# Attention with mixture of experts on one core: attended values kept by feature, normalised by quads of heads, and three rotating PSUM banks

## What is computed

```
xn  = layernorm(x)
Q, K, V = split_heads(xn @ Wq.T), ..., 16 heads of 32
S   = where(causal, Q @ K.T / sqrt(32), -1e30)
att = (softmax(S) @ V, heads side by side) @ Wo.T
ffn = routed experts (2 of 8, width 352) + shared MLP (width 704), both on xn
out = x + att + ffn
```

## Time and profile before

| | us |
|---|---|
| median of 3 runs (1117.13 to 1122.85) | 1117.6 |
| the profiled execution's own time | 1127.01 |
| its span, first to last instruction | 1125.0 |
| PE busy in the span | 1046.2 |
| DVE, ACT, POOL busy | 784.6, 637.9, 506.4 |

### The profile page before, as it was taken

One profiled execution on the slowest core, in us unless ns is written; L12 is line 12 of the kernel. 1 busy time (PEld: TensorE's weight loads), 2 busy tenths in 40 slices (PEclk: granted clock), 3 DMA queues, 4 the chain that ended last, 5 costly groups with the idle time before them and its releaser, 6 DMA issues. The chain is left out here.

```text
span 1125.0 us, 18890 instructions
## 1 busy us (share of the span) xinstructions
PE 1046.2 (93%) x5379; PEld 817.6 (73%) x5380; DVE 784.6 (70%) x1675; ACT 637.9 (57%) x1278; POOL 506.4 (45%) x568
## 2 busy tenths in 40 slices
PE   6999979888899998999999999998989999999994
PEld 4767867666677776777778777776867777778872
DVE  6732324565688887788888888865568888888872
ACT  3323211265588786787787887872155555565550
POOL 0013903388756564556566565651013443333321
PEclk9999989988899999999999999998989999999997
DMA  6989996255543553644445426118789444443432
GB/s 213 322 335 361 136 293 231 94 67 102 132 133 77 150 148 75 163 118 136 115 113 151 126 64 191 45 39 266 243 283 278 90 76 75 75 72 68 71 54 35
DMA packets 106201, 163.61 MB, mean 145 GB/s; under 512 B 53984, under 2 KB 64480, under 8 KB 102656
## 3 DMA queue, kind: packets, MB, share of 16 engines
q1 hardware_dynamic: 95776, 141.82, 44.1%
q0 software_dynamic: 9760, 20.49, 10.0%
q10 hardware_dynamic: 576, 0.26, 0.1%
HBM read 101.25 MB, written 61.28 MB: 144 GB/s over the span
## 5 line engine op out<-in xcount | busy, mean ns | idle before, releaser
L1198 POOL TENSOR_TENSOR prob_lo<-prob,prob_hi 128x512 fp32r<-128x512 f32 (+2 forms) x320 | 308.3, 977 | 203.3 <-ACT prob_hi L1243 147.0
L1236 ACT ACTIVATE prob<-ps_s 128x512 f32<-128x512 f32 (+3 forms) x384 | 188.0, 490 | 127.1 <-PE ps_s L1463 77.1
L1243 ACT ACTIVATE prob_hi<-prob 128x512 fp32r<-128x512 f32 (+3 forms) x384 | 198.6, 517 | 12.4 <-ACT row_stage L1217 12.4
L1862 DVE TENSOR_TENSOR rw_lo<-gu_sb,rw_hi 128x704 fp32r<-128x704 f32 x156 | 138.8, 893 | 52.7 <-ACT rw_hi L1806 47.7
L1306 DVE CUSTOM_DVE_ANT_0 ps_m<-ps_m,causal 128x384 f32<-128x384 f32 (+3 forms) x256 | 126.7, 495 | 69.2 <-PE ps_m L1432 66.9
L1806 ACT ACTIVATE rw_hi<-gu_sb 128x704 fp32r x156 | 123.5, 794 | 62.8 <-PE ps_ru L1895 43.6
L1458 PE MATMUL ps_s<-qs,ks 97*128 97x512 f32 (+3 forms) x384 | 140.4, 366 | 9.4 <-ACT prob L1236 9.2
L1779 POOL DMA_INDIRECT out<-work,slot_table x39 | 63.5, 1627 | 181.1 <-DVE work L1847 148.2
L1481 PE MATMUL ps_o<-prob_hi,vs 128*66 128x512 f32 (+3 forms) x384 | 133.1, 347 | 10.4 <-issue 9.6
L1432 PE MATMUL ps_m<-ks,qs 96*128 96x512 f32 (+3 forms) x384 | 139.1, 362 | 0.6 <-DVE maxima L1306 0.2
L1483 PE MATMUL ps_o<-prob_lo,vs 128*66 128x512 f32 (+3 forms) x384 | 132.0, 344 | 0.0
(11 more groups left out here) (201 smaller groups left out, 2353.0 us busy)
## 6 DMA issues: line engine op xcount, KB each, us to landing
xt<-xt_blocks SPq DMA_DIRECT2D x7, 2048.0 KB, 9.1
v_rows<-work SPq DMA_DIRECT2D x16, 512.0 KB, 3.0
xt_blocks<-xt SPq DMA_DIRECT2D x4, 2048.0 KB, 11.3
qk_hi<-work SPq DMA_DIRECT2D x8, 1024.0 KB, 4.7
qk_lo<-work SPq DMA_DIRECT2D x8, 1024.0 KB, 7.5
qs<-qk_hi SPq DMA_DIRECT2D x64, 128.0 KB, 2.9
ks<-qk_hi SPq DMA_DIRECT2D x64, 128.0 KB, 3.2
vs<-v_rows SPq DMA_DIRECT2D x32, 256.0 KB, 4.7
```

What stands on the lines that cost most here:

```text
L1198: nc.gpsimd.tensor_tensor(prob_lo[:, s % NPL, 0:w], prob[:, s % NP, 0:w], prob_hi[:, s % NPH, 0:w].bitcast(F32), ALU.subtract).then_inc(lo ...
L1236: nc.scalar.activation(prob[:, s % NP, 0:w], ps_s[s % NS][:, 0:w], ACT.Exp, scale=SCALE).then_inc(exp_done, 1)
L1243: nc.scalar.activation(prob_hi[:, s % NPH, 0:w], prob[:, s % NP, 0:w], ACT.Copy).then_inc(hi_ready, 1)
L1862: nc.vector.tensor_tensor(w_lo[:, k, :], chunk(e, k), w_hi[:, k, :].bitcast(F32), ALU.subtract).then_inc(w_lo_ready, 1)
```

## The change

Attended values stay as they come out of `ps_o`, by feature, so nothing is turned back.

- `work` is seen as [feature of four heads, token tile, quad of heads, token]. At the end of each half SP moves the copy by DMA: 32 rows of high part into `work`, 32 of low part into `o_low`, and the row of sums to a table in DRAM (`place_output`, PLACE = VALUE + 2).
- When the four heads of a quad are through, a half at a time, `class Finish` works on all 128 partitions: SP loads the 2048 sums as 128x16 (`load_sums`, VALUE + 4), DVE inverts them (`invert`, VALUE + 6), SP stores them (`save_inverses`, VALUE + 7) and spreads each over 32 partitions with four broadcast DMAs (`spread_inverses`, VALUE + 9), DVE adds the low parts (`sum_outputs`, VALUE + 10) and multiplies (`normalize`, VALUE + 11). There are 16 of these; the last is done in `out_phase`, which uses the tiles it touches last. Heads go by quads of one batch (`head_of`).
- `turn_o`, its four instructions on DVE, and `turn` and `copy` of `out_phase` are gone. `hi` and `lo` there read `work` itself.
- The bank `ps_x` is free: scores and the turned maxima now take three banks in turn (`bank`, `wait_bank_read`).
- Wo is loaded and split during the last steps of attention. `out_phase` is written out without loops.
- SP goes step by step, and its loads hang on steps instead of heads (`XT_AT`, `STORE_AT`, `BASE_AT`, `RAW_AT`). V has two slots instead of four. The planner no longer counts 270 for `turn_o`.

```diff
-    COPY, TURN, NORM = VALUE + 1, VALUE + 2, VALUE + 3
+    COPY, PLACE = VALUE + 1, VALUE + 2
+    SUMS, INVERT, SAVE, SPREAD, SUM, NORM = [VALUE + n for n in (4, 6, 7, 9, 10, 11)]
...
-        if 0 <= s - TURN < STEPS and (s - TURN) % NB in ENDS:
-            cost += 270
...
+    XT_AT = {step_of(unit - 1, UP_END[-1] - 1) + 1: unit for unit in range(1, UNITS)}
+    RAW_AT = {NB: 0, **{s + 2: ks[0] + 1 for s, ks in SPLIT_AT.items() if ks[0] + 1 < NF}}
...
-        NS = 2
+        NS = 3
+        uses = [use for s in range(ALL) for use in (
+            ([("score", s - AHEAD)] if 0 <= s - AHEAD < STEPS else [])
+            + ([("row", (s - ROW) // NB)] if 0 <= s - ROW < STEPS and (s - ROW) % NB == 0 else []))]
...
+                def place_output(s):
...
+                    sp.wait_ge(o_copied, 2 * g + half + 1)
+                    if n == 0:
+                        wait(sp, finish.o_ready, 2 * (g // QUAD - 1) + half + 1)
...
+                    for into, rows in ((attended[at, tiles, h // QUAD, :], slice(0, DK)),
+                                       (halves[half].low[at], slice(DK, 2 * DK))):
+                        sp.dma_start(into, o_copy[rows, half, :].rearrange("p (a q) -> p a q", a=4)
+                                     ).then_inc(finish.o_placed[half], 16)
...
+                    sp.dma_start(sums_dram[k:k + 1, n * TBW:(n + 1) * TBW],
+                                 o_copy[2 * DK:2 * DK + 1, half, :]).then_inc(finish.sums_saved[half], 16)
...
                 def copy_o(s):
...
-                    wait(act, o_turned, o - 1)
+                    wait(act, finish.o_placed[half], 32 * g)
+                    wait(act, finish.sums_saved[half], 16 * g)
...
+                    for lag, stage in ((INVERT, finish.invert), (SUM, finish.sum_outputs),
+                                       (NORM, finish.normalize)):
+                        if finished(s - lag):
+                            stage(dve, quad_half(s - lag))
...
-                    for lag, stage in ((TURN, turn_o), (0, maximum), (ROW, turn_row)):
+                    for lag, stage in ((0, maximum), (ROW, turn_row)):
...
+class Finish:
+    def load_sums(self, sp, k):
+        sp.wait_ge(self.sums_saved[k % 2], 16 * QUAD * (k // 2 + 1))
...
+    def invert(self, dve, k):
+        dve.wait_ge(self.sums_loaded[k % 2], 16 * (k // 2 + 1))
...
+    def save_inverses(self, sp, k):
+        sp.wait_ge(self.inverted, k + 1)
...
+    def spread_inverses(self, sp, k):
+        sp.wait_ge(self.inv_saved[k % 2], 16 * (k // 2 + 1))
...
+    def normalize(self, dve, k):
+        dve.wait_ge(self.o_summed, k + 1)
+        dve.wait_ge(self.inv_spread[k % 2], 16 * QUAD * (k // 2 + 1))
```

More of the change, by code:

```diff
@@ L20 @@
 from concourse import mybir
+from collections import namedtuple
 from contextlib import ExitStack
@@ L50 @@
 HEAD_SLOTS = 4
+V_SLOTS = 2
+QUAD = P // DK
+QT = S // P
 W_SLOTS = 4
@@ L97, in moe_attention_kernel @@
     slots_dram = nc.dram_tensor("slots", [NSLOT, 2], F32, kind="Internal").ap()
+    sums_dram, inv_dram = [nc.dram_tensor(name, [2 * B * H // QUAD, QUAD * TBW], F32, kind="Internal").ap()
+                           for name in ("sums", "inverses")]
     xt_dram = nc.dram_tensor("xt_blocks", [NTB, P, 2, KC, TBW], F32, kind="Internal").ap()
@@ L1216, in row @@
                     wait(act, row_saved, 16 * (g - HS + 1))
-                    nc.scalar.activation(row_stage[:, c, :], ps_row[0:QT, :], ACT.Copy,
+                    nc.scalar.activation(row_stage[:, c, :], bank("row", g)[0:QT, 0:P], ACT.Copy,
                                          scale=-1.0).then_inc(row_ready, 1)
@@ L1235, in exp @@
                     wait(act, lo_pool, count(LO_POOL, s - NP))
-                    nc.scalar.activation(prob[:, s % NP, 0:w], ps_s[s % NS][:, 0:w], ACT.Exp,
+                    nc.scalar.activation(prob[:, s % NP, 0:w], bank("score", s)[:, 0:w], ACT.Exp,
                                          scale=SCALE).then_inc(exp_done, 1)
@@ L1440, in turn_row @@
                     pe.wait_ge(max_ready, g + 1)
-                    wait(pe, row_ready, g)
-                    wait(pe, o_read, turned["outputs"])
-                    nc.tensor.transpose(ps_row[0:QT, :], maxima[:, c, 0:QT],
+                    wait_bank_read(pe, "row", g)
+                    nc.tensor.transpose(bank("row", g)[0:QT, 0:P], maxima[:, c, 0:QT],
                                         ident[:, :]).then_inc(row_turned, 1)
-                    turned["rows"] += 1
                 def score(s):
@@ L1454, in score @@
                         pe.wait_ge(row_loaded[g % 2], 16 * (g // 2 + 1))
-                    wait(pe, exp_done, s - NS + 1)
+                    wait_bank_read(pe, "score", s)
                     q0 = qb * TBW + first
                     diagonal = s % NB in DIAGONAL
-                    last = nc.tensor.matmul(ps_s[s % NS][:, 0:w],
+                    last = nc.tensor.matmul(bank("score", s)[:, 0:w],
                                             ks[0:ROWS + 1, c, kt * P:(kt + 1) * P],
@@ L1462, in score @@
                     if diagonal:
-                        last = nc.tensor.matmul(ps_s[s % NS][:, 0:P], eye[:, :], late[:, :],
+                        last = nc.tensor.matmul(bank("score", s)[:, 0:P], eye[:, :], late[:, :],
                                                 start=False, stop=True)
@@ L1484, in value @@
                                      stop=n in ENDS).then_inc(pv_done, 1)
-                def turn_o(s):
-                    if s % NB not in ENDS:
-                        return
-                    o = 2 * (s // NB) + BLOCKS[s % NB][0]
-                    pe.wait_ge(o_copied, o + 1)
-                    wait(pe, o_read, o)
-                    wait(pe, row_ready, turned["rows"])
-                    for q in range(4):
-                        last = nc.tensor.transpose(ps_ot[:, q, 0:VW], o_copy[:, o % 2, q * P:(q + 1) * P],
-                                                   ident[0:VW, 0:VW])
-                    last.then_inc(o_turned, 1)
-                    turned["outputs"] += 1
                 def gate_or_up(unit, m):
@@ L1656, in lo, with last_outputs @@
                     wait(dve, hi_ready, t + 1)
-                    nc.vector.tensor_tensor(a_lo[:, c % R], ps_t[c % R][:, :, :],
+                    nc.vector.tensor_tensor(a_lo[:, c % R], tile_of(t),
                                             a_hi[:, c % R].bitcast(F32),
                                             ALU.subtract).then_inc(lo_ready, 1)
+                def last_outputs(i, c):
+                    t = U * i + c
+                    if t == 1:
+                        finish.invert(dve, LAST)
+                    if t == 5:
+                        finish.sum_outputs(dve, LAST)
+                    if t == 6:
+                        finish.normalize(dve, LAST)
                 def add(i, c):
```

327 lines of the change are left out of this document (183 added, 144 removed).

## The result

The changed kernel takes 1136.2 us in the median of four runs (1132.5 to 1141.0), the one before 1118.6 in runs on the same chip; the ratio is 1.0145 (95% interval 1.0106 to 1.0183). So it is **1.45% slower**, where 1102 us and a faster kernel had been forecast.

A forecast was written before the change was run, and what follows sets the result against it. PE was taken to bound most of attention and the output product, POOL the early heads. Terms 17.7 + 9 - 14 + 0 + 3 gave +15.7 us: 1111.3 from the profiled 1127.0, put at 1102 for the median, range 1083 to 1127.

The forecast's parts named there:

- term 3: Chain of Finish in attention: late inverses hold DVE, the maxima's reads and PE beyond a 15.7 us limit; 14 us lost.
- What bounds the kernel: PE sets the pace from 305 to 758 us and in the output product; POOL does from 233 to 305.
- 1. The transposes (+17.7): Attention from 305 to 758 us: PE saves 0.31 us for each of 57 groups of turn_o transposes, 17.7 us gained.
- rival C: Attention: PE was not the only bound, two thirds of the transposes' gain are lost, 1114 us; chance 0.14.
- 2. The raw weights (+9): Attention: earlier raw weights save 4.7 us of PE idle and 3.6 of clock, with small gains 9 us together.
- The collisions: Chains beside large transfers: 7 us for two behind input blocks, 3 at the second quad's sums, 2 at the shared MLP's sum.
- B: Attention: chain transfers land like their neighbours and hold DVE and PE; slower from about 3.2 us, 1136 at 3.5; chance 0.17.
- Rival A: Attention: the chain is hidden, small DMAs slip past large ones; 1090 us, or 1085 with the seam; chance 0.24.
- 4. The seam (0): Attention to output product: ready Wo is offset by the last quad's chain; 0, from +5 to -4 us.
- 5. The output product (+3): Output product: 15 tiles save 0.42 us each, 6.3 us, less a residual tile 2.5 to 3 us late; net 3 gained.
- 6. DVE's new operations (0): Attention: 32 wide operations, 48 us at most, fit in DVE's 77 us free; nothing lost.

The follow-up runs named there:

- Experiment 9: Kernel with the product seven steps later, second and third raw weights issued later: at steps 158 and 170 0.988, at 160 and 173 0.990 of the kernel before.
- experiment 8: Changed kernel with two banks for the scores again and the turned maxima in a third of their own: 1133.6 us, 1.015 of the kernel before.
- experiment 5: Changed kernel with the next head's six loads three steps later, behind the spreading of the inverses: 1118.8 us, 0.996 of the kernel before.
- experiment 1: Changed kernel without the chain of the sums, so the output is not divided: 1096.7 us, 0.974 of the kernel before.
- experiment 6: Changed kernel, two block loads and a group of residual loads moved off the chains: 1131.3 us, 1.010 of before; with later head loads too 1112.9 us, 0.991.
- experiments 4: Changed kernel with the next head's six loads behind the chain's stages in SP's step, instead of ahead: 1134.2 us, 1.012 of the kernel before.

## Why the prediction was wrong

The step that failed is term 3, the cost of the chain: 14 us were put on it and it took 35.0 between the marks.

**What bounds the kernel** held: PE in attention and the output product, POOL up to head 6, where nothing was gained (102.4 and 102.0 us).

**1. The transposes (+17.7)** were right. Between the marks the kernel without the chain is 19.6 faster than before; 3.7 of that lies with the raw weights (next), and 15.9 in 25 heads are 0.64 a head, where 2 x 0.31 = 0.62 was worked out. That nearly all of it came also leaves no room for rival C, another bound behind PE.

**2. The raw weights (+9)** were sized too high. Before, heads 11 to 15 took 72.5 us, 10.9 over undisturbed ones; without the chain 66.8, 7.2 over theirs. The difference is 3.7. What came back is the clock. These are heads 11 to 15, before and without the chain:

```profile
404.90:477.42 72.52, 65.98 (x352) 50.66 (x351) 57.57 (x142) 53.00 (x121) 38.00 (x40) 0.95 0.52 130
```

```profile
398.70:465.50 66.80, 60.15 (x320) 46.56 (x319) 52.03 (x113) 53.03 (x121) 41.15 (x41) 1.00 0.46 127
```

PE is busy 4.3 us longer than in four undisturbed heads before and 0.6 us without the chain: 3.7 us, as the forecast's 3.6 for the clock. But it is idle for 6.5 us before and for 6.6 without the chain, so the 4.7 us of idle time counted as gained were not. No wait for the weights is among them now; PE stands for the values' bank (3.6 us, put down to nothing that the profile shows) and for the maxima (3.0), in heads in which ACT and DVE also split weights. That the splitting is the cause was not tested. Experiment 9 shows a wait of 5.5 us costing about itself. What the third bank is worth stays open (experiment 8).

**3. The chain (-14) is the step that failed.** It costs 35.0 us between the marks. The mechanism was the forecast's own, DVE held at its place until a landing, the reads of the maxima behind it and PE with them, and the limit was right: 15.7 us after the copy begins, and DVE came to the product 15.4 us after it (591.41 - 2.91 - 573.08). Two sizes were wrong.

The first is the length of the chain: "landed 15.7. Just on the limit: I count 0.3 us in each of seven, 2 us". In the half shown above it landed at 18.3, in the other five that waited at the product at 19.8 to 21.5. Piece by piece in the half shown, from the copy's start, with the forecast's times in parentheses: the third issue came at 3.4 us (1.8), because SP was still spreading the first half's inverses, but that cost nothing, since the sums had landed at 6.7 and DVE came to them only at 9.4 (8.2). The inverses were ready at 9.6. Their store was issued at 10.8 (9.3), when the six head loads were through, and landed by 14.9 (12.3): 4.1 us with six head loads just issued, where the estimate had 3.0, taken from a head's loads among themselves. The fourth spreading was issued by 16.6 (13.7) and landed at 18.3 (15.7). So two pieces, 1.5 and 1.1 us, make the 2.6, and with a limit of the chain's own length every us goes through. With the loads behind the spreading (experiment 5) the store goes out at 9.6, and in this half the product begins at 15.3 without a wait.

The second is what a us of standing costs. The forecast had "Each us beyond is one lost" and 2 us for the clock, at the two block loads alone. Measured are 19.4 us of PE's idle time and 15.5 of slower matmuls (experiment 1), 0.8 for each us.

The collisions were right in kind. Of the two chains whose spreading stands behind an input block one has the longest wait, 5.69 us, but the other only 1.19 (3.4 each were forecast); the block ahead of the second quad's sums cost DVE 2.20 (3); and one wait of 4.54 stands beside the stores and loads of the shared MLP's sum, where 2 us were given to two chains. Taking two of the blocks and that group of loads away gave back 4 us alone and 11 with the head loads moved (experiment 6); 12 were forecast for all collisions.

**The rival that came** is B, and only in part as written. It was to decide "from about 3.2 us" for all landings; the medians in attention are 2.1 us for the spreading, 2.8 for the store of the inverses and 2.9 for the sums. By its own condition it would not have come about, so that its 1136 us for landings of 3.5 us is the measured time is luck. What it lacked was the queue: order and issues, landings that are long just where the queue is full (1.4 to 4.1 us for the store of the inverses). A limit "just met" was evidence for B, not for the forecast, and 0.17 was too little. Rival A is out by the 11 chains of attention in which DVE waits.

**4. The seam (0)**: +2.0, within its bounds. The first Wo matmul comes 36.2 us after the last mark, 36.1 before, but the forecast ended the seam when the first tile is through: 42.6 us after the mark before (771.21 - 728.60), 40.7 now (774.90 - 734.25). PE's idle time was 7.3 us, not 9, and DVE's wait for the spreading was in it:

```profile
768.10 0.69 DVE L273 TENSOR_TENSOR work<-work,o_inv 128x512 f32<-128x512 f32 x1 [4.48 <-DMA o_inv<-inverses]
```

**5. The output product (+3)**: -3.6 from the first tile to the experts' first transpose (49.3 us before, 52.9 now), which with the seam's 2.0 makes 1.6 us lost. The tile was right, 2.72 us against 2.77, as these starts show:

```profile
797.76 0.69 DVE L1790 TENSOR_TENSOR y_tile<-ps_ay,y_tile 128x512 f32<-128x512 f32 x1 [1.36 <-PE ps_ay L1804]
...
800.48 0.69 DVE L1790 TENSOR_TENSOR y_tile<-ps_ay,y_tile 128x512 f32<-128x512 f32 x1 [1.36 <-PE ps_ay L1804]
```

What was undersized is the residual tile behind a whole expert in the DMA engines, to which a faster product also comes sooner: 2.5 to 3 us were counted for one, and there were two. DVE waited 7.23 us there and PE 4.53, and 4.89 and 2.19 at the second expert:

```profile
786.43 0.69 DVE L1790 TENSOR_TENSOR y_tile<-ps_ay,y_tile 128x512 f32<-128x512 f32 x1 [7.23 <-DMA y_tile<-out]
```

```profile
787.78 0.80 PE L1804 MATMUL ps_ay<-wo_hi,a_hi 128*128 128x512 f32 x1 [4.53 <-DVE a_lo L1773]
```

**6. DVE's new operations (0)**: its waits, not its work, are the price. The kernel with the late product has all of these operations and takes 388.4 us between the marks, 5.1 more than the one without the chain, which has the 16 additions but none of the 16 products. The forecast took 15 us for the most that an exclusion of DVE and POOL could cost at the products; these 5.1 leave room for no more than that. What the additions cost was not tested. (The Trainium skill, SBUF — State Buffer, "SBUF: two separate sides", states such an exclusion for an operation of DVE with two SBUF inputs against one of GpSimd that reads SBUF. Whether it acted here no run shows.)

## What to carry to other kernels

A chain of small DMAs with a compute engine at a fixed place at its end costs every us by which it is later than that place, and here 0.8 us more for each of them in slower matmuls, so a chain computed to end "on the limit" is a chain that is late. Look for who really needs the result (here the next quad needed the sum of two parts, not the product), and put the last step where nobody waits. And read the queue that issues the chain row by row, with every landing taken for the state that the queue is in there: moving six issues by three steps was worth 1.9%.

## What was not expected of the hardware

The same store of 8 KB landed 4.1 us after its issue with six head loads issued just ahead of it, and 1.4 us with them behind (experiments 4 and 5). And a residual tile of 256 KB issued behind an expert's four loads (at 775.49) landed after 10.8 us, where the median from 771 to 819 us was 3.3 before, though the DMA engines' mean share in the output product was 0.80:

```profile
773.30:827.00 53.70, 46.27 (x187) 36.95 (x185) 21.30 (x32) 8.84 (x14) 2.15 (x3) 0.93 0.80 246
```
